# Six-layer stack of local attention and feed-forward: the norms of q and k made apart, the gelu behind the copy of V, and a shorter variance step

## The reference

```python
for i in range(6):                       # DEPTH
    x = attn_layer(shift_tokens(x), Wqkv[i], q_scale[i], k_scale[i], Wo[i]) + x
    x = ffn_layer(shift_tokens(x), ln_g[i], ln_b[i], W1[i], b1[i], W2[i], b2[i]) + x

# attn_layer: 16 heads of 64, windows of 32 that look one window back
q = t / max(norm(t), 1e-12) * qs         # l2norm per head; the same for k
q = q * cos * scale + rotate_half(q) * sin * scale
out = softmax(mask(8 * q @ k.T)) @ v;  return out @ Wo
# ffn_layer
xn = (x - mu) / sqrt(var + 1e-05) * g + bln
a, gate = split(xn @ W1 + b1);  return a * gelu(gate) @ W2 + b2
```

## Time and profile before

| | |
|---|---|
| median of 3 runs | 4276.08 us (4270.42 to 4289.24) |
| profiled execution | 4277.94 us |
| its span, first to last instruction | 4276.2 us |
| busy in the span | TensorE 3789.2 us (89%), VectorE 3357.8 us (79%), ScalarE 2526.5 us (59%), GpSimd 2501.7 us (59%) |
| mean granted TensorE clock | 0.971 of full speed |
| instructions | 153902 |

### The profile page before, as it was taken

The page is one execution under the profiler, slowest core; times in us unless marked ns, Lnnn a source line. Parts: engine busy times, 40 slices in busy tenths (PEclk is TensorE's granted clock), DMA queues, the critical chain, the costliest instruction groups (busy, mean ns, idle before and its releaser), DMA issues. The chain is left out here.

```text
span 4276.2 us, 153902 instructions
## 1 busy us (share of the span) xinstructions
PE 3789.2 (89%) x67640; PEld 2277.3 (53%) x67640; DVE 3357.8 (79%) x4385; ACT 2526.5 (59%) x3236; POOL 2501.7 (59%) x2036
## 2 busy tenths in 40 slices
PE   6887799999999999999678886899999999999996
PEld 3232456666666666666333333566666666666664
DVE  7998788888888888888354436788888888888884
ACT  5886456666666666666223453566566665666664
POOL 0001677777787777876100005787777877777772
PEclk8999999999999999999789998999999999999998
DMA  0001232323323223222000002323323233232221
GB/s 20 1 1 42 67 87 67 91 72 79 89 67 91 73 78 90 64 70 62 17 1 1 1 1 78 90 74 85 78 73 89 73 84 80 74 88 71 69 63 40
DMA packets 165604, 260.98 MB, mean 61 GB/s; under 512 B 58574, under 2 KB 79818, under 8 KB 164938
## 3 DMA queue, kind: packets, MB, share of 16 engines
q1 hardware_dynamic: 164936, 251.13, 22.5%
HBM read 48.61 MB, written 1.05 MB: 12 GB/s over the span
## 5 line engine op out<-in xcount | busy, mean ns | idle before, releaser
L1382 POOL TENSOR_TENSOR f_k_rotated<-f_rope_ak,f_rope_bk 128x1024 f32<-128x1024 f32 x192 | 454.1, 2365 | 271.6 <-DVE f_rope_bk L1432 271.6
L1098 PE MATMUL banks<-f_wqkv,H 128*128 128x512 f32 x1152 | 561.7, 611 | 23.2 <-DVE f_rope_bk L1432 12.2
L1098 PE MATMUL banks<-f_wqkv,G 128*128 128x512 f32 x1152 | 552.9, 602 | 1.0 <-issue 1.0
L1364 POOL MEMSET f_kT<- 128x256 f32 x2 | 0.6, 312 | 840.5 <-POOLq L514 461.1
L1382 POOL TENSOR_TENSOR f_q_rotated<-f_rope_aq,f_rope_bq 128x1024 f32<-128x1024 f32 x192 | 454.9, 2369 | 52.9 <-DVE f_rope_bq L1432 52.6
L1155 PEld LDWEIGHTS banks<-f_O_T,f_wo 128*128 128x128 f32 x3072 | 372.5, 192 | 106.0 <-issue 93.2
L1322 ACT ACTIVATE f_V<-banks 128x1024 f32<-128x1024 f32 x192 | 196.0, 1021 | 377.6 <-PE banks L1098 377.6
L1155 PE MATMUL banks<-f_O_T,f_wo 128*128 128x128 f32 x3072 | 375.4, 275 | 11.0 <-issue 8.4
L1429 DVE TENSOR_TENSOR f_rope_aq<-banks,f_rope 128x1024 f32<-128x1024 f32 x192 | 235.0, 1224 | 184.7 <-ACT f_sqq L1287 169.2
L1394 POOL TENSOR_TENSOR f_q_rotated<-f_q_rotated,f_inverse_norm 128x1024 f32<-128x1024 f32 x192 | 365.5, 1903 | 15.0
L1376 POOL TENSOR_TENSOR f_E<-f_E,f_row_inverse 128x1024 f32<-128x1024 f32 x192 | 367.9, 1916 | 8.0 <-DVE f_row_inverse L1464 8.0
(11 more groups left out here) (207 smaller groups left out, 9075.0 us busy)
## 6 DMA issues: line engine op xcount, KB each, us to landing
f_P_T_paired<-f_P_T SPq DMA_DIRECT2D x1536, 64.0 KB, 2.0
f_V_previous<-f_V SPq DMA_DIRECT2D x192, 384.0 KB, 3.9
f_V_previous<-f_V SPq DMA_DIRECT2D x192, 128.0 KB, 2.5
f_wqkv<-in_L_ffn_Wqkv SPq DMA_DIRECT2D x48, 384.0 KB, 3.7
f_rope<-in_rope SPq DMA_DIRECT2D x24, 512.0 KB, 4.2
f_wo<-in_L_ffn_Wo SPq DMA_DIRECT2D x12, 512.0 KB, 5.5
f_w<-in_L_ffn_W SPq DMA_DIRECT2D x12, 341.0 KB
f_w<-in_L_ffn_W SPq DMA_DIRECT2D x24, 64.0 KB
```

Source lines behind the costliest of these rows:

```text
L1098: mm = nc.tensor.matmul(ps[:, o * BLK:(o + 1) * BLK], xs, w[:, c * INNER + o * BLK:c * INNER + (o + 1) * BLK], start=True, stop=True)
L1382: nc.gpsimd.tensor_tensor(qk[i][:], ra[i][:], rb[i][:], ALU.add).then_inc(radd.sem, 1)
```

## The change

It has three parts, all in the stack. (1) The sums of squares of q and of k are clamped apart, each right behind its own sum on VectorE, and times -0.5; ScalarE makes Ln, Exp and the Square of the seed for q behind the square of k, and for k where both were; GpSimd does for q, and then for k: sum of the rotated parts, three Newton instructions of 16 columns in place of four of 32, scaling. (2) In kind 3, ScalarE loads the gelu's table, copies V, and then does the gelu. (3) For the variance, ScalarE adds a Square over 128x512, GpSimd has one product in place of four instructions, and VectorE scales xn with two fused instructions in place of one.

```diff
         def _(act):
...
+            def seeds(n, i):
+                h = slice(i * HEADS, (i + 1) * HEADS)
+                act.wait_ge(clamped.sem, clamped.at(n, i + 1))
+                act.wait_ge(newton.sem, newton.past(n - 1, 3 * (i + 1)))
+                nc.scalar.activation(lg[:, h], ss[n % 2][:, h], ACT.Ln, scale=-2.0).then_inc(seeded.sem, 1)
+                act.wait_ge(seeded.sem, seeded.at(n, 3 * i + 1))
+                nc.scalar.activation(y0[:, h], lg[:, h], ACT.Exp, scale=-0.5).then_inc(seeded.sem, 1)
+                act.wait_ge(seeded.sem, seeded.at(n, 3 * i + 2))
+                nc.scalar.activation(lg[:, h], y0[:, h], ACT.Square).then_inc(seeded.sem, 1)
...
                 if live(s):
                     squares(n, 1, k_mm, PK)
-                if (b := feed(s, 11)) is not None:
-                    act.wait_ge(f_gev.sem, f_gev.at(blk(b)))
-                    nc.scalar.activation(ge[:].rearrange("p j t -> p (j t)"), ge[:].rearrange("p j t -> p (j t)"),
-                                         ACT.Gelu).then_inc(f_ge.sem, 1)
+                    seeds(n, 0)
+                if feed(s, 11) is not None:
+                    nc.scalar.preload_act_table_set("gelu_and_others")
                 if live(s):
...
                     nc.scalar.activation(V[n % 4][:], PV_F, ACT.Copy).then_inc(v_ev.sem, 1)
-                if feed(s, 11) is not None:
+                if (b := feed(s, 11)) is not None:
+                    act.wait_ge(f_gev.sem, f_gev.at(blk(b)))
+                    nc.scalar.activation(ge[:].rearrange("p j t -> p (j t)"), ge[:].rearrange("p j t -> p (j t)"),
+                                         ACT.Gelu).then_inc(f_ge.sem, 1)
                     nc.scalar.preload_act_table_set("natural_log_exp_and_others")
...
                 if live(s):
-                    act.wait_ge(clamped.sem, clamped.at(n))
-                    act.wait_ge(newton.sem, newton.past(n - 1))
-                    nc.scalar.activation(lg[:], ss[n % 2][:], ACT.Ln).then_inc(seeded.sem, 1)
-                    act.wait_ge(seeded.sem, seeded.at(n, 1))
-                    nc.scalar.activation(y0[:], lg[:], ACT.Exp, scale=-0.5).then_inc(seeded.sem, 1)
+                    seeds(n, 1)
                 if (b := feed(s, 8)) is not None:
...
-                    nc.scalar.activation(xsq[:], var[:], ACT.Ln).then_inc(f_seed.sem, 1)
+                    nc.scalar.activation(xsq[:], var[:], ACT.Ln, scale=-2.0).then_inc(f_seed.sem, 1)
                     act.wait_ge(f_seed.sem, f_seed.at(blk(b), 1))
+                    act.wait_ge(f_xn.sem, f_xn.past(blk(b) - 1))
                     nc.scalar.activation(vy0[:], xsq[:], ACT.Exp, scale=-0.5).then_inc(f_seed.sem, 1)
+                    act.wait_ge(f_seed.sem, f_seed.at(blk(b), 2))
+                    nc.scalar.activation(xsq[:], vy0[:], ACT.Square).then_inc(f_seed.sem, 1)
...
         def _(pool):
...
                     for i, t in enumerate((qT_mm, kT_mm)):
+                        h = slice(i * HEADS, (i + 1) * HEADS)
                         pool.wait_ge(rot.sem, rot.at(n, 3 * (i + 1)))
                         pool.wait_ge(t.sem, t.past(n - 1))
                         nc.gpsimd.tensor_tensor(qk[i][:], ra[i][:], rb[i][:], ALU.add).then_inc(radd.sem, 1)
-                    pool.wait_ge(seeded.sem, seeded.at(n))
-                    nc.gpsimd.tensor_tensor(rt[:], y0[:], y0[:], ALU.mult).then_inc(newton.sem, 1)
-                    pool.wait_ge(newton.sem, newton.at(n, 1))
-                    nc.gpsimd.tensor_tensor(rt[:], rt[:], ss[n % 2][:], ALU.mult).then_inc(newton.sem, 1)
-                    pool.wait_ge(newton.sem, newton.at(n, 2))
-                    nc.gpsimd.tensor_scalar(rt[:], rt[:], -0.5, 1.5, ALU.mult, ALU.add).then_inc(newton.sem, 1)
-                    pool.wait_ge(newton.sem, newton.at(n, 3))
-                    nc.gpsimd.tensor_tensor(rn[:], rt[:], y0[:], ALU.mult).then_inc(newton.sem, 1)
-                    pool.wait_ge(newton.sem, newton.at(n))
-                    pool.wait_ge(radd.sem, radd.at(n))
-                    for i in range(2):
-                        nc.gpsimd.tensor_tensor(heads_of(qk[i][:]), heads_of(qk[i][:]),
-                                                over(rn[:, i * HEADS:(i + 1) * HEADS], DH), ALU.mult)\
+                        pool.wait_ge(seeded.sem, seeded.at(n, 3 * i + 3))
+                        nc.gpsimd.tensor_tensor(rt[:, h], lg[:, h], ss[n % 2][:, h], ALU.mult).then_inc(newton.sem, 1)
+                        pool.wait_ge(newton.sem, newton.at(n, 3 * i + 1))
+                        nc.gpsimd.tensor_scalar(rt[:, h], rt[:, h], 1.5, None, ALU.add).then_inc(newton.sem, 1)
+                        pool.wait_ge(newton.sem, newton.at(n, 3 * i + 2))
+                        nc.gpsimd.tensor_tensor(rn[:, h], rt[:, h], y0[:, h], ALU.mult).then_inc(newton.sem, 1)
+                        pool.wait_ge(newton.sem, newton.at(n, 3 * i + 3))
+                        pool.wait_ge(radd.sem, radd.at(n, i + 1))
+                        nc.gpsimd.tensor_tensor(heads_of(qk[i][:]), heads_of(qk[i][:]), over(rn[:, h], DH), ALU.mult)\
                             .then_inc(nrm.sem, 1)
                 if (b := feed(s, 8)) is not None:
                     pool.wait_ge(f_seed.sem, f_seed.at(blk(b)))
-                    nc.gpsimd.tensor_tensor(xsq[:], vy0[:], vy0[:], ALU.mult).then_inc(f_nt.sem, 1)
...
-                    nc.gpsimd.tensor_tensor(var[:], xsq[:], vy0[:], ALU.mult).then_inc(f_nt.sem, 1)
+                    pool.wait_ge(f_xn.sem, f_xn.past(blk(b) - 1))
+                    nc.gpsimd.tensor_tensor(var[:], xsq[:], var[:], ALU.mult).then_inc(f_nt.sem, 1)
...
         def _(dve):
...
             def sums(n, i):
...
                     .then_inc(red.sem, 1)
+                dve.wait_ge(red.sem, red.at(n, i + 1))
+                h = ss[n % 2][:, i * HEADS:(i + 1) * HEADS]
+                nc.vector.tensor_scalar(h, h, 1e-24, -0.5, ALU.max, ALU.mult).then_inc(clamped.sem, 1)
...
                     sums(n, 1)
-                    dve.wait_ge(red.sem, red.at(n))
-                    nc.vector.tensor_scalar(ss[n % 2][:], ss[n % 2][:], 1e-24, None, ALU.max).then_inc(clamped.sem, 1)
...
-                    nc.vector.tensor_scalar(var[:], bank(5), EPS, None, ALU.add).then_inc(f_eps.sem, 1)
+                    dve.wait_ge(f_xn.sem, f_xn.past(blk(b) - 1))
+                    nc.vector.tensor_scalar(var[:], bank(5), EPS, -0.5, ALU.add, ALU.mult).then_inc(f_eps.sem, 1)
...
-                    nc.vector.scalar_tensor_tensor(xn[:], xcs[:], vec[b // NBLK % 2][:, 0:1], var[:], ALU.mult, ALU.mult)\
+                    nc.vector.scalar_tensor_tensor(xn[:], xcs[:], vec[b // NBLK % 2][:, 0:1], vy0[:], ALU.mult, ALU.mult)\
                         .then_inc(f_xn.sem, 1)
+                    dve.wait_ge(f_xn.sem, f_xn.at(blk(b), 1))
+                    nc.vector.scalar_tensor_tensor(xn[:], var[:], 1.5, xn[:], ALU.add, ALU.mult).then_inc(f_xn.sem, 1)
```

14 lines of the change are left out of this document (4 added, 10 removed).

## The result

The changed kernel takes 4306.32 us, the median of 5 runs (4292.70 to 4309.95), beside 4276.08 us before (5 runs, 4270.42 to 4289.24): a ratio of 1.0057, 95% interval 1.0044 to 1.0070. It is slower by about 0.6%, 30 us, where 1.7%, 73 us, was forecast. The profiled execution of it took 4292.70 us (span 4290.8), the shortest of its five, so the two profiled executions differ by 14.8 us only.

A forecast was written before the change was run, and what follows sets the result against it. TensorE, 95% busy in steady layers, was taken as the bound, VectorE next. 48 groups at +1.54 us gave +74; with -3 starts, +10 rope products, -10 transfers, +71 on 4277.94: 4349 us, range 4245 to 4435.

The forecast's parts named there:

- the sum: Whole kernel: four slots take 67.2 us, 1.54 above 65.66, times 48 groups gives +74 us; smaller terms make it +71.
- The gain: TensorE's wait for k's scaling goes in kinds 0 to 2: four slots at 61.5 us, 4.1 of 65.66 gained.
- The clamp of q: On VectorE, q's clamp is locked out by GpSimd's sum in nearly every slot: 1.3 us each, 64.5 for four slots.
- in most slots, over 0.7 us each: Sign to look for: TensorE waits behind VectorE's subtraction in most slots, over 0.7 us each.
- Kinds 3 and 0: q's seeds before the table load delay V's copy and k's scaling: kind 3 takes 15.7 (+0.2), kind 0 16.75 (+0.4).
- Kinds 1 and 2: ScalarE's Square delays q's rotation, kind 1 17.55 us (+1.2); VectorE's extra scaling makes kind 2 start late, 17.2.
- The second scaling: Two scalings of xn on VectorE in kind 1 add 0.70 us; kind 2 starts 0.85 late.
- The case of it standing behind k's scaling: Xn's second scaling blocked by GpSimd's scaling of k: 17.2 becomes about 18.6; part of a 4426 us rival, chance 0.15.
- The variance's gain on GpSimd: In kind 0, GpSimd losing three of four variance instructions is worth nothing, as it then waits for the next row inverse.
- The clamps behind rope products: Ten times, rope products on GpSimd come just ahead of a slot, q's clamp may wait 1.9 us longer: +10 us.
- the lock is there, the three additions fall in slack: Rival: q's clamp is blocked, but half of the three additions cost nothing: about 4285 us, chance 0.17.
- The rival without a lock: Rival: q's 16-column clamp takes no lock against GpSimd, TensorE is the bound, four slots 62.4: 4168 us, chance 0.13.

The follow-up runs named there:

- kernel 2: The changed kernel without any clamp, the floor 1e-24 added inside Ln and -0.5 back on GpSimd: 4132.7 us, ratio 0.9660.
- kernel 5: kernel 2 with an idle VectorE tensor_reduce of 128x16 where each clamp stood: 4158.3 us, ratio 0.9718.
- kernel 10: kernel 2 with the old variance step (four GpSimd instructions, no Square on ScalarE, one scaling of xn): 4138.2 us, ratio 0.9664.
- kernel 4: The changed kernel with the old variance step (four GpSimd instructions, no Square on ScalarE, one scaling of xn): 4295.6 us, ratio 1.0042.
- kernel 11: kernel 2 with only the variance's Square moved from ScalarE to GpSimd as a product: 4110.6 us, ratio 0.9600.
- kernel 7: The kernel before, with weight and rope table loads of layers 2 to 5 cut to a sliver: 4267.1 us, ratio 0.9977.
- kernel 1: The changed kernel with q's clamp one VectorE instruction later, behind the first product of k's rotation: 4313.8 us, ratio 1.0087.
- kernel 8: The changed kernel with weight and rope table loads of layers 2 to 5 cut to a sliver: 4304.1 us, ratio 1.0058.
- kernel 6: The changed kernel with the gelu ahead of the copy of V again: 4350.0 us, ratio 1.0170.
- kernel 3: The kernel before, with its one 32-column clamp split into two of 16, each behind its own sum: 4310.1 us, ratio 1.0081.
- kernel 9: The kernel before without its one clamp, the floor 1e-24 added inside Ln: 4253.0 us, ratio 0.9938.

## Why the forecast was right in its direction and wrong in its size

The step that failed is **the sum**: "1.54 above 65.66" for each of "48 groups of four". The runs show 0.91 us per group in its place, in 40 groups. The base, 65.66, was one group that lies 1.2 us below the mean, and eight of the 48 groups are no steady ones; behind that, a delay was put in the wrong slot, and the shorter variance step on GpSimd, "worth nothing", was worth something.

**The gain** is right: TensorE's wait for the scaling of k goes in all kinds but 0 (37.7 to 12.1 us), and kernel 2 shows what it is worth.

**The clamp of q** is right to a few hundredths: 1.3 us forecast, 1.325 measured; what the lock takes, 64.5 - 61.5 = 3.0 us per group, against (2712.1 - 2600.4) / 40 = 2.8 between the change and kernel 5. VectorE's idle time before the k rotation, 52.4 us in 79 slots before, is 1.1 us in the whole kernel. The subtraction became a gate, but "in most slots, over 0.7 us each" is too much: it holds matmuls in 62 of the 160 steady slots, 36 of kind 1 (0.71 us in the mean), 22 of kind 2 (0.42) and 4 of kind 0; in kind 3 the copy of V comes last.

**Kinds 3 and 0** are right: 15.7 and 16.75 forecast, 15.81 and 16.82 the medians (16.09 and 16.89 the means). The copy of V holds TensorE 0.60 us in the slot shown (0.85 forecast).

**Kinds 1 and 2**: 34.75 us together forecast, 34.83 the means, but in the wrong slot. The rotation of q in kind 1 is late, at T+2.41 (median; T+1.59 before, forecast T+2.55). But I let the late VectorE of kind 1 delay the rotation of kind 2. The residual add (L1524) is behind both scalings of xn in VectorE's order, and the q transposes of the next slot wait for it; so kind 1 itself gets longer, 18.19 us, and kind 2 starts in step, its rotation at T+1.42. The sum of the two was right, and in part by luck: the mechanism was wrong. With it the 67.2 for four slots, beside medians of 67.14, is in part luck too.

**The second scaling** took 0.69 us (L1511) in all 48 cases, behind nothing. The case of it standing behind k's scaling did not occur in the change. The rule behind that case was sound: in kernel 10 the scaling of xn, with its two inputs in SBUF, stands behind GpSimd's sum of k in 44 of 48 cases (1.86 us in place of 0.71).

**The variance's gain on GpSimd, "worth nothing"** is wrong. Kernels 4 and 10 show that the four instructions there, with the meetings that they bring about, cost about as much as the Square and the second scaling; two of them, without the Square on ScalarE, are better than either (kernel 11 is 22 us under kernel 2). The step rested on GpSimd's wait for the row inverse behind the variance. Already the trace of before shows no such wait: in kind 1, P times the inverse starts without a gap in 40 of 40 slots, and so does the sum of q behind it, at T+7.42 (median). In the change the sum of q starts at T+4.91, in kernel 4 at T+6.25.

**The sum** is where the size was lost. The forecast multiplied 67.2 - 65.66 = 1.54 by 48 groups. (a) The base was one group. 67.2 is the sum of medians after (67.14); but the medians of before add up to 66.00, 0.34 above it. It wasn't even the shortest: 30 of 154 stretches of four steady slots are shorter, down to 64.66. (b) On top of its medians, before carried 66.89 - 66.00 = 0.89 us in the mean, after only 67.80 - 67.14 = 0.66, so 0.23 less. The transfers make a part of that at most: TensorE's wait ahead of `values` fell from 38.8 to 32.7 us over the steady slots, 0.15 per group, and kernel 7, with fewer loads, still lies 0.89 above its medians. The rest stays open. In sum 0.91 per group, not 1.54: over ten layers 36.6 us, not 62. (c) There are 40 steady groups, not 48. I gave the other eight 12 us, less 3 for the starts of the calls: +9. In the profiled pair the starts gained 12.0 us and the stretch between 8.1. In three relatives of the change (kernels 1, 4, 8) the starts are 2 to 5 us shorter than before, in a fourth (kernel 6) 3.5 longer, so most of the 12.0 is the luck of this execution; the stretch between is 594 to 598 us in all kernels with the norms apart and clamps, against 601 to 606 in kernels 3, 7, 9 and before.

Where that gain of some 6 us comes from, the traces show in part. From the last first q transpose of call 1 to the first instruction of the softmax attention pass 83.7 us before (2020.03 to 2103.69) and 76.4 in the change (2035.37 to 2111.73): 82 to 85 in all six kernels with the old variance step (before, 3, 4, 7, 9, 10), 76 to 79 in all seven with the new one or kernel 11's. In this drain the variance step is made twice. GpSimd's four instructions take 4.4 us from start to end each time; the Square and the one product take 2.0 in the change, and the second scaling 0.7, so the step itself is 1.8 us shorter. Kernel 4 differs from the change in this step alone: the change is 1.8 us ahead of it when the first xn is scaled, 4.7 at the second, and 5.6 at the end. Some 3.6 of that is the step, twice; the rest, beside a granted clock of 0.86 in this drain of the change, 0.80 in kernel 4 and 0.76 before, stays open. The forecast had put the drain at nothing.

(d) The clamps behind rope products, "+10", cost about 2: next section. With the starts between -5 and +4 and the stretch between at -6, the +9 became about -2 to -11. So the forecast's +71 loses 25 by (a) and (b) and 11 to 20 by (c), while its -10 for transfers, which is part of (b), and its +10 for the rope products cancelled: +26 to +35, beside the 30 measured. The 36.6 in it comes from the one profiled execution of the change, the shortest of its five, so that the sum comes out so well is no proof.

The rival that came nearest, "the lock is there, the three additions fall in slack" (4285), was wrong in its reason: the additions did not fall in slack (kinds 1 and 3 are longer). The rival without a lock (4168) gave nearly the time of kernel 5, 4158, in which the lock is missing and little else differs.

## What to carry to other kernels

Where VectorE and GpSimd are both busy most of the time, ask of each small instruction whether its form excludes the other engine: a clamp of 16 columns cost 1.3 us a slot, and taking both out of the change gained 4%, more than five times what the change had lost. Moving such an instruction by a microsecond changed only whom it met (kernel 1), and speeding up or slowing down a neighbour can bring about a new meeting (kernels 4 and 10); fold it into an activation's bias, or use a form that doesn't exclude. And take the base of a difference from the median or mean of all steady groups, not from one that looks clean, and count only the groups that are steady.

## What the runs showed of the hardware that was not expected

Behind the rope products GpSimd has two long instructions back to back, P times the inverse and the sum of q. A clamp tried in the first was expected to be in danger of waiting through both. VectorE, then GpSimd, in the change:

```profile
939.83 1.56 DVE L1445 TENSOR_SCALAR f_sum_of_squares<-f_sum_of_squares 128x16 f32<-128x16 f32 x1
```

```profile
939.44 1.92 POOL L1387 TENSOR_TENSOR f_E<-f_E,f_row_inverse 128x1024 f32<-128x1024 f32 x1
941.32 2.37 POOL L1394 TENSOR_TENSOR f_q_rotated<-f_rope_aq,f_rope_bq 128x1024 f32<-128x1024 f32 x1
```

The clamp ends at 941.39, 0.03 us behind the first instruction's end, although the second is recorded from 941.32. All ten such clamps end 0.03 to 0.04 us behind it (1.36 to 1.56 us long), and so do 54 clamps of q in kernel 4: the waiting VectorE instruction gets in between two of GpSimd's, and a wait through most of both was not seen. A clamp that is tried just as the second begins does wait for all of that one. It happened once, in kernel 6; VectorE, then GpSimd:

```profile
447.61 2.37 DVE L1444 TENSOR_SCALAR f_sum_of_squares<-f_sum_of_squares 128x16 f32<-128x16 f32 x1
```

```profile
445.74 1.91 POOL L1386 TENSOR_TENSOR f_E<-f_E,f_row_inverse 128x1024 f32<-128x1024 f32 x1
447.61 2.35 POOL L1393 TENSOR_TENSOR f_q_rotated<-f_rope_aq,f_rope_bq 128x1024 f32<-128x1024 f32 x1
```

Also, the size of the blocked instruction made no difference here: 16 columns are blocked for the full rest of GpSimd's 2.36 us, as 32 were in the earlier trace rows, while a reduce over the same 16 columns took 0.17 us in all 384 cases.
